# Turning gathered token rows in an expert FFN: TensorE transposes and ScalarE copies replaced by a transposing DMA

## The reference

```python
x = x + _L0_xattn_ref(_layernorm(x), ctx_1024, ...)          # 16 heads, 77 keys, softmax minus lambda * softmax
h = _layernorm(x).reshape(-1, 256)                            # 2048 tokens
probs = softmax(h @ gate_w.T); w, idx = top_k(probs, 2); w = w / sum(w)
combine = zeros((T, 8)).at[arange(T)[:, None], idx].add(w)
for e in range(8):                                            # I = 1024
    g, u = split(h @ gate_up_proj[e].T, 2)
    out += combine[:, e, None] * (silu(g) * u @ down_proj[e].T)
x = x + out
```

## Time and profile before

| what | us |
|---|---|
| median of 3 runs | 607.62 |
| their range | 602.35 to 608.39 |
| the profiled execution | 606.88 |
| its span, first to last instruction | 605.2 |
| up to the first expert matmul | 288.06 |
| slots 0 to 5, with the second stream of weights | 114.49 |
| slots 6 to 13 | 160.20 |
| slot 14 and its last `down` | 25.65 |
| the last results turned back and scattered | 16.80 |

### The profile page before, as it was taken

One profiled execution on the slowest core, in us unless ns is written; L12 is line 12 of the kernel. 1 busy time (PEld: TensorE's weight loads), 2 busy tenths in 40 slices (PEclk: granted clock), 3 DMA queues, 4 the chain that ended last, 5 costly groups with the idle time before them and its releaser, 6 DMA issues.

```text
span 605.2 us, 12286 instructions
## 1 busy us (share of the span) xinstructions
PE 500.8 (83%) x3882; PEld 372.3 (62%) x3897; DVE 394.6 (65%) x803; ACT 349.2 (58%) x653; POOL 272.5 (45%) x347
## 2 busy tenths in 40 slices
PE   5667989999998877013888999989999999999980
PEld 3444656766766545002667787768777887777750
DVE  5345568988886554892589888865656656655541
ACT  2211778977887862001797887756566556555540
POOL 4016547556654532003226554654555555644244
PEclk9995899999998885557899999999999999999995
DMA  7558476777585311401257666643243223322223
GB/s 237 183 154 232 150 223 157 232 225 203 170 248 177 125 52 67 126 0 35 76 155 169 161 158 161 164 122 45 53 72 52 55 46 62 53 55 44 27 27 43
DMA packets 57626, 72.55 MB, mean 120 GB/s; under 512 B 18712, under 2 KB 42904, under 8 KB 57432
## 3 DMA queue, kind: packets, MB, share of 16 engines
q1 hardware_dynamic: 46048, 56.03, 30.6%
q0 software_dynamic: 11520, 15.74, 15.4%
HBM read 49.08 MB, written 22.41 MB: 118 GB/s over the span
## 4 chain that ended last, share of the span: by engine, by line
PE 57%; DVE 13%; DMA 9%; ACT 9%; issue 6%; SPq 3%; POOL 3%; ACTq 0%; POOLq 0%; DVEq 0%
PE bank L1274 21%; PE bank L1290 11%; PE bank L1095 4%; PE bank L1141 4%; PE bank L1127 3%; DMA out<-FB,slot_tok 2%; DMA FB<-w 2%; PE bank L1150 2%; PE bank L1245 2%; DVE FB L1038 2%; DVE FB L1034 2%; PE bank L1164 2%; PE bank L1301 2%; PE bank L1176 2%; PE bank L1109 2%
## 5 line engine op out<-in xcount | busy, mean ns | idle before, releaser
L1274 PE MATMUL bank<-FB,WE 128*128 128x0 bf16 x1440 | 188.7, 281 | 1.2 <-ACT FB L745 1.2
L1274 PEld LDWEIGHTS bank<-FB,WE 128*128 x1440 | 137.3, 98 | 30.6 <-issue 2.1
L1034 DVE TENSOR_TENSOR FB<-FB,bank 128x512 f32<-128x512 f32 x120 | 82.4, 687 | 105.3 <-ACT FB L752 104.1
L613 POOL DMA_INDIRECT out<-FB,slot_tok x60 | 95.7, 1596 | 102.6 <-DVE FB L1046 93.8
L752 ACT ACTIVATE FB<-bank 128x512 f32<-128x512 f32 x120 | 71.7, 598 | 101.7 <-PE bank L1274 90.4
L1290 PE MATMUL bank<-FB,WE 128*128 128x0 bf16 x720 | 104.2, 280 | 12.8 <-DVE FB L1038 9.9
L604 POOL DMA_INDIRECT FB<-x_parts,slot_tok x60 | 64.4, 1073 | 99.5 <-PE bank L1245 47.1
L1290 PEld LDWEIGHTS bank<-FB,WE 128*128 x720 | 63.9, 97 | 41.5 <-issue 26.7
L1038 DVE TENSOR_TENSOR FB<-FB 128x512 bf16<-128x512 f32 x120 | 82.3, 686 | 0.0
L539 POOL TENSOR_TENSOR WE<-FB,WE 128x256 bf16<-128x256 f32 x104 | 68.4, 685 | 23.0 <-ACT WE L644 23.0
L758 ACT ACTIVATE FB<-FB 128x512 bf16<-128x512 f32 x120 | 74.9, 624 | 0.2 <-DVE FB L1034 0.2
(11 more groups left out here) (170 smaller groups left out, 649.2 us busy)
## 6 DMA issues: line engine op xcount, KB each, us to landing
FB<-w SPq DMA_DIRECT2D x26, 512.0 KB, 5.4
WE<-w SPq DMA_DIRECT2D x44, 256.0 KB, 3.2
WE<-q_parts SPq DMA_DIRECT2D x32, 200.0 KB
WE<-x SPq DMA_DIRECT2D x16, 256.0 KB, 5.3
q_parts<-FB SPq DMA_DIRECT2D x32, 128.0 KB
x_parts<-WE SPq DMA_DIRECT2D x20, 128.0 KB, 3.8
out<-WE SPq DMA_DIRECT2D x20, 128.0 KB, 5.5
q_parts<-WE SPq DMA_DIRECT2D x16, 128.0 KB
```

The lines of the kernel that those rows point to most:

```text
L613: pool.indirect_dma_start(out=out, out_offset=bass.IndirectOffsetOnAxis(ap=slot_tok[:, c:c + 1].bitcast(U32), axis=0), in_=y_sb[c % 2], in ...
L1034: nc.vector.tensor_tensor(hid[k % 2], hid[k % 2], up_bank[k % 2][1][:, :], ALU.mult).then_inc(h_ready, 1)
L1274: ins = nc.tensor.matmul(to, wf[:, bass.ds(at + o, P)], xgT[s % 2][:, 2 * part + kc, :].shape_from_register(long[s % 2]), start=(z == 0), ...
```

## The change

The transposes of L1245 and the copies of L745 are gone, with PSUM bank 6's part in them. In their place SP issues for each tile one DMA with `transpose=True` that reads `xg[c % 2]` as 128 partitions x 4 blocks x 128 and writes `xgT[s % 2]` as 128 partitions x 4 blocks x 128 columns of the tile's place. It waits for the gather of the tile, and from slot 2 on for all `up` of slot s-2 (`g_mm`). GpSimd's gather of tile c now waits for the turn of tile c-2, and `up` of a slot's step 0 waits for all four turns of that slot. The turns are put into SP's queue between the loads of the second stream.

```diff
+            def turn_tile(s, i):
+                c = SUB * s + i
+                sp.wait_ge(xg_in[c % 2], 16 * (c // 2 + 1))
+                if s >= 2:
+                    sp.wait_ge(g_mm, FC * (s - 1))
+                sp.dma_start(xgT[s % 2][:, :, i * P:(i + 1) * P], xg[c % 2].rearrange("p (k f) -> p k f", k=4), transpose=True).then_inc(xg_turned[c % 2], 16)
+
+            def park_in():
+                sp.wait_ge(split_out, 64)
+                sp.wait_ge(late_lo, len(LATE))
+                sp.dma_start(WE[:, E - 1, 2 * W1N:EW], wd).then_inc(parked_in, 16)
-            for j in range(len(LATE)):
+            for j in range(LSTG):
                 load_late(j)
-            sp.wait_ge(split_out, 64)
-            sp.wait_ge(late_lo, len(LATE))
-            sp.dma_start(WE[:, E - 1, 2 * W1N:EW], wd).then_inc(parked_in, 16)
+            sp.wait_ge(idx_ready, 1)
+            for i in range(SUB):
+                turn_tile(0, i)
+            for k in range(FC * (NS - 1)):
+                if k % FC < SUB:
+                    turn_tile(k // FC + 1, k % FC)
+                if LSTG + k < len(LATE):
+                    load_late(LSTG + k)
+                if k == len(LATE):
+                    park_in()
...
             def gather(c):
                 if c >= 2:
-                    pool.wait_ge(xgt_mm, c - 1)
+                    pool.wait_ge(xg_turned[c % 2], 16 * (c // 2))
...
-            def xgT_copy(s, half):
-                act.wait_ge(xgt_mm, SUB * s + 2 * half + 2)
-                if s >= 2:
-                    act.wait_ge(g_mm, FC * (s - 1))
-                nc.scalar.activation(xgT[s % 2][:, :, 2 * half * P:2 * (half + 1) * P].rearrange("p c (i n) -> p i c n", i=2),
-                                     in_bank[:, :].bitcast(BF16).rearrange("p (i c n) -> p i c n", i=2, c=4), ACT.Copy).then_inc(xgT_ready, 1)
...
-                    if c in (3, 6) and s + 1 < NS:
-                        xgT_copy(s + 1, c // 6)
...
-            def turned_rows(s, half):
-                if 2 * s + half > 0:
-                    pe.wait_ge(xgT_ready, 2 * s + half)
-                for i in range(2):
-                    pe.wait_ge(xg_in[i], 16 * (2 * s + half + 1))
-                    A = in_bank[:, 256 * i:256 * (i + 1)].bitcast(BF16)
-                    for c in range(4):
-                        ins = nc.tensor.transpose(A[:, c * P:(c + 1) * P], xg[i][:, c * P:(c + 1) * P], ident[:, :])
-                    ins.then_inc(xgt_mm, 1)
...
                 if c == 0:
-                    pe.wait_ge(xgT_ready, 2 * s + 2)
+                    for i in range(2):
+                        pe.wait_ge(xg_turned[i], 16 * SUB // 2 * (s + 1))
...
-            turned_rows(0, 0)
-            turned_rows(0, 1)
...
-                    if c in (2, 5) and s + 1 < NS:
-                        turned_rows(s + 1, c // 5)
```

More of the change, by code:

```diff
@@ L190, in moe_attention_kernel @@
         A5, A6, A7 = bank[5], bank[6], bank[7]
-        up_bank, y_bank, in_bank, turn_bank = [bank[0:2], bank[2:4]], bank[4:6], bank[6], bank[7]
+        up_bank, y_bank, turn_bank = [bank[0:2], bank[2:4]], bank[4:6], bank[7]
         QROWS = 3 * HD + 2
@@ L271, in moe_attention_kernel @@
         rconst_ready = sem("rconst_ready")
-        xgt_mm = sem("xgt_mm")
-        xgT_ready = sem("xgT_ready")
+        xg_turned = [sem(f"xg_turned{p}") for p in range(2)]
         g_mm = sem("g_mm")
@@ L771, in _ @@
             act.wait_ge(idx_ready, 1)
-            xgT_copy(0, 0)
-            xgT_copy(0, 1)
             for s in range(NS):
```

## The result

The changed kernel takes 617.86 us in the median (617.58 to 618.92, 4 runs) against 606.12 (602.35 to 608.39) for the kernel before on the same chip: a ratio of 1.018, with a 95% interval of 1.014 to 1.023. It is slower by 1.8%, clear of the noise; whether by as much as 2% the interval leaves open. The profiled execution took 617.65, with a span of 615.9.

What follows compares the result with a forecast made beforehand. TensorE was taken to bound slots 4 to 13, and TensorE, DVE and ScalarE together slots 1 to 3. 6.2 + 3.1 + 8.2 + 0.3 - 7.4 = +10.4 us on 606.88 gave 617.3; 8-in-10 range 600 to 665.

Steps and rivals of the forecast that it cites:

- L: Time from issue to landing of one transposing DMA; taken as 4.5 us, bounded by 2.9 and 8.6.
- The way in: Ahead of slot 0: two turns with a gather between, nothing covering them; loss 2L - 2.8 = 6.2 us.
- Slot 0: In slot 0: second turn waits for a load released 8.2 us in; 20.7 against 17.56, loss 3.1 us.
- Slots 1 to 4: Turn, gather, turn chain, started late by SP's queue, takes 21.3 us, longer than each slot; losses 8.2 us together.
- loads reach ScalarE late: Load behind the third turn in SP's queue lands a microsecond later; near nothing at L = 4.5, growing with L.
- Slot 5: In slot 5: only the first turn is behind a load; chain 20.4 us against 20.07, loss 0.3 us.
- the fallen clock: A TensorE stop long enough to lower its clock would add time; no size given, not in the sum.
- Slots 6 to 13: No loads, so turns land in time; removed transposes save 0.92 us a slot, 7.4 us gained.
- The sum: Whole kernel: losses less the late gain come to +10.4 us, giving 617.3 us.
- Rival (a): Turns hide behind the slots at L = 2.9, kernel faster: 599 us; decides below L of 3.25, chance 0.14.
- (b): Turns throughout as quick as a plain copy, L = 3.8: no change, 608 us; chance 0.28.
- (c): Turns bound all slots, even late ones, at L = 8.6: 715 us; chance 0.21 above 6, including element-by-element writing.

Runs made afterwards that it cites:

- e10_clock: Changed kernel plus 14 matmuls into an unused PSUM bank before TensorE's wait in slots 2 to 5, timed beside the unedited changed kernel; 614.95 us, ratio 1.012.
- e7_four: Changed kernel with four transposing DMAs of 128x128 for each tile in place of one with three-dimensional operands; 718.76 us, ratio 1.185.
- e4_pe_first: Changed kernel with slot 0's rows turned by TensorE and ScalarE as before the change, the others by DMA; 614.49 us, ratio 1.013.
- e1_order: Changed kernel with the turns placed earlier among the loads in SP's queue, nothing else; 603.9 us, ratio 0.995.
- e6_clock: Changed kernel plus 14 matmuls into an unused PSUM bank before TensorE's wait in slots 2 to 5, first timing; 618.28 us, ratio 1.015.
- e3_pe_until_7: Changed kernel with TensorE and ScalarE turning the rows for slots 0 to 6, DMA those for 7 to 14; 599.33 us, ratio 0.984.
- e8_order_small: Changed kernel with earlier turns in SP's queue and 40 of 44 second-stream loads cut to an eighth (some weights wrong); 600.26 us, ratio 0.990.
- e9_changed: The changed kernel itself, no edit, timed again beside e10_clock; 617.01 us, ratio 1.016 to the kernel before.

## Why the prediction was right, and where not

The forecast of 617.3 us and its sign were right, and so was the main mechanism, the turn that stands behind a load in SP's queue; some of the terms were off, in both directions.

- **L, taken as 4.5 us everywhere.** It is 2.8 us with nearly empty queues, of which SP's 1.2 for the instruction are a part, so the way in was mis-sized by it. In slots 1 to 4 it is 3.1 to 5.9; the landings that e10_clock records there are 2.9 to 5.9, 4.1 in the mean, so 4.5 was near. The count behind it held: 512 blocks to a tile. The nearest row, 3.8, was too high for the quiet case and too low for the last turn beside the loads. The Trainium skill gives about 1.3 us for a 128x128 transpose through the DMA (VectorE: DVE Perf Modes, The three transpose paths). The prediction's estimate of four times this figure doesn't hold for a DMA with four blocks: all four landed within 2.8 us. The figure is close to the 1.23 us that SP is held by a DMA of one block in e7_four; whether it counts the same thing no run here shows.
- **The way in, 6.2 us.** Measured 2.9. The formula 2L - 2.8 was right: with 2.8 for L it gives 2.8. e4_pe_first took the two turns out of this way and got 2.7 us back.
- **Slot 0, 3.1 us.** Measured 19.02 - 17.56 = 1.5. The landings were quicker than 4.5, but the second turn went out 9.3 us into the slot and not 8.2.
- **Slots 1 to 4, 8.2 us by a chain that SP's queue starts too late.** The mechanism was right, and e1_order shows it: reordering that queue alone takes 15.7 us off slots 0 to 5. The size was not: 13.7 us. Three things were left out or set to nothing. The release itself comes later: in slot 1 it is the 6.3 us of the prediction, but 8.0, 8.1 and 7.5 in slots 2 to 4, which start after a stop. Where e10_clock fills the stop and the clock stays at 1.00, the release in these slots is at 6.5 to 6.8; it doesn't separate the stop from the clock. The last turn takes 5.9 in slot 2, with three loads behind it. And loads reach ScalarE late by 4.6 us in three places, which I had called near nothing. In slot 2 the 2.4 us beyond the forecast are 1.7 of release, 1.4 of the last landing and 0.4 of gather, less 1.1 for the second turn's quicker landing.
- **Slot 5, 0.3 us.** Measured 0.9; by e10_clock and e6_clock it is the fallen clock that takes the gain away, a term that was named but not in the sum.
- **Slots 6 to 13, -7.4 us.** Slots 7 to 13 gave -6.0, and -6.5 in e3_pe_until_7, where 7 x 0.92 is 6.4. Slot 6 lost 1.8. There DVE waits until 422.5 for a scatter, for 3.0 us, and TensorE behind it for 2.8; before the change it was 2.0 and 1.8. That is 1.0 us more, and what follows shows the rest: the 12 matmuls of the next `up` take 2.46 us where the step ahead of the stop took 1.50, and the granted clock of the slot is 0.92 for 1.00 before. In e1_order TensorE waits 2.5 us in the same place, the clock stays at 1.00, and slot 6 lasts 20.5 us, less than before the change. The wait itself begins with a scatter issued 0.3 us ahead of the 1 MB of `w_parts` at 415.20; in e10_clock the same scatter, issued 0.1 us ahead of it, lands after 7.5 us, against 3.8 for the median scatter of slots 7 to 13 in e3_pe_until_7. That this traffic is the cause fits, and wasn't tried.
- **The sum.** +10.4 forecast; the terms measured are 2.9 + 1.5 + 13.7 + 0.9 - 4.3, and -0.3 for what follows slot 13: +14.4 in the profiled expert parts, +11.7 between the medians. The hit to within a microsecond is in part luck, twice over. The way in and slot 0 were over by 4.9, while slots 1 to 4 were under by 5.5, slot 5 by 0.6 and slots 6 to 13 by 3.1; and the 4 us that this leaves in the profile are made up for by the part ahead of the expert loop, which was 3.7 us shorter by chance.
- **Rival (a), a quick turn.** Its condition, L below 3.25, was met on the way into slot 0, and its reasoning about the late slots was right. (By its own sum the chain fits into slot 1, 18.20 us, only at L below 3.0.) It failed because L is longer where the chain is tight, and the release later. The nearest to its world is e8_order_small, all turns by DMA and little traffic, at 600.3 us where it had put 599; but that took the new order too, and the small loads alone stayed at 606.0. The 599.3 of e3_pe_until_7 is no test of it, since TensorE turns the rows of slots 0 to 6 there.
- **Rivals (b) and (c).** With a mean landing of 4.1 us beside the loads the 3.8 of (b) was almost as near as 4.5; its 608 us fails by the later release and the late loads. No landing reached the 6 us above which (c) starts.

What stays open: how much of the later landing beside the loads is the load queued ahead of a turn, how much the loads behind it, and how much GpSimd's gathers and scatters. They were not separated. Open too is whether e1_order's order and e3_pe_until_7's late turns would add up; no run joins them.

## What to carry to other kernels

Moving work from a full engine to a DMA moves it into a queue: before costing the transfer, ask what stands ahead of it there and when that is released. With two buffers the chain of transfer, refill, transfer must fit into one period; two terms that each push it over are not two losses, and mending either is nearly enough. And a change can be right for one part of a loop alone: here the DMA turn gained 0.9 us a slot once the weight stream was over, and cost three or four microseconds in each of slots 1 to 4 beside it.

## What the hardware showed that was not expected

- A transposing DMA holds SP for 1.2 us (60 instructions, median 1200 ns) against 0.33 for a plain load, and it is the same for one block of 128x128 (median 1232 ns) as for four.
- Four blocks, 128 KB, land 2.4 us after the issue starts with nearly empty queues, and what waits for them starts at 2.8; beside 256 KB loads the landing is up to 5.9. (The 3.8 us of a plain 128 KB copy in the earlier trace rows is a median in the traffic of the whole span, so it is no measure of which kind is quicker.)
- Stops of TensorE of 2.9 to 4.1 us ahead of slots 2, 3 and 5 were followed by matmuls at a lower clock (granted 0.92 and 0.93 in the slot), those of 1.7 and 2.2 us ahead of slots 1 and 4 were not (1.00). Behind the stop ahead of slot 3 an `up` took 2.40 us for 12 matmuls that take 1.46 later in the slot, the same matmuls at a lower one of the two levels (1.2 and 2.4 GHz) for part of the time. The length of the stop alone doesn't tell: e9_changed has two of 2.1 us, with 1.00 after the one and 0.92 after the other. In e10_clock, with stops of at most 0.7 us there, the granted clock was 1.00 in all four slots.
